# Message products inside the edge batches, node rows fetched per edge type

## The reference

```python
Ks, Qt, Vs = (K[src], Q[tgt], V[src])
for t in range(ET):
    mask = edge_types == t
    Ke = jnp.einsum('ehd,dk->ehk', Ks, Wa[t])
    Ve = jnp.einsum('ehd,dk->ehk', Vs, Wm[t])
    scores = jnp.sum(Ke * Qt, -1) * inv_sqrt_dk * relation_pri[t]
    scores = jnp.where(mask[:, None], scores, -jnp.inf)
    w = jax.nn.softmax(scores, axis=0)
    msgs = msgs + jnp.where(mask[:, None, None], w[..., None] * Ve, 0.0)
agg = jax.ops.segment_sum(msgs.reshape(-1, OUT_DIM), tgt, num_segments=n)
out = agg + node_features      # then a layer norm over the 256 features
```

## Time and profile before

| | us |
|---|---|
| three runs | 1167.97, 1186.32, 1187.55 |
| median | 1186.32 |
| profiled execution, time | 1167.97 |
| its span, first to last instruction | 1167.3 |

### The profile page before, as it was taken

One profiled execution on the slowest core, in us unless ns is written; L12 is line 12 of the kernel. 1 busy time (PEld: TensorE's weight loads), 2 busy tenths in 40 slices (PEclk: granted clock), 3 DMA queues, 4 the chain that ended last, 5 costly groups with the idle time before them and its releaser, 6 DMA issues.

```text
span 1167.3 us, 18084 instructions
## 1 busy us (share of the span) xinstructions
PE 967.1 (83%) x5053; PEld 677.5 (58%) x5053; DVE 803.3 (69%) x1708; ACT 587.4 (50%) x1534; POOL 640.5 (55%) x818
## 2 busy tenths in 40 slices
PE   5989999997157788777877878778778898999998
PEld 4767777775034444444444444444444687888886
DVE  7755888885256777777767677776767677887541
ACT  2657999983234554555545455554555322322220
POOL 4516788886725666666656666565664025664000
PEclk9999999999565766666667666666776799999999
DMA  9722544444736776766767767677674274210020
GB/s 294 220 71 104 159 145 145 146 146 174 234 114 182 208 212 210 205 204 203 214 202 214 210 198 211 201 211 208 201 211 146 69 226 152 79 46 19 1 86 25
DMA packets 112091, 189.89 MB, mean 163 GB/s; under 512 B 18187, under 2 KB 80734, under 8 KB 111990
## 3 DMA queue, kind: packets, MB, share of 16 engines
q0 software_dynamic: 38992, 129.87, 36.1%
q1 hardware_dynamic: 69718, 55.57, 15.7%
q10 hardware_dynamic: 3280, 3.28, 0.8%
HBM read 154.21 MB, written 34.44 MB: 162 GB/s over the span
## 4 chain that ended last, share of the span: by engine, by line
PE 55%; ACT 12%; issue 11%; another core or an unknown queue 10%; DVE 9%; DMA 1%; SPq 1%; POOL 0%; DVEq 0%; ACTq 0%; POOLq 0%
PE ps L2364 7%; PE ps L1621 7%; PE ps L2351 7%; PE ps L1604 6%; PE ps L921 4%; ACT edge L1500 4%; PE ps L2315 3%; PE ps L932 2%; PE ps L909 2%; PE ps L960 2%; ACT edge L1488 2%; PE ps L985 2%; ACT edge L1485 1%; PE ps L1639 1%
## 5 line engine op out<-in xcount | busy, mean ns | idle before, releaser
L1425 POOL DMA_INDIRECT big<-kv_scratch,src_i x336 | 317.8, 946 | 203.0 <-issue 89.8
L1604 PE MATMUL ps<-edge 64*128 64x256 f32 x784 | 177.6, 595 | 39.0 <-issue 38.8
L1750 DVE TENSOR_TENSOR big<-big,ps 128x1024 f32<-128x1024 f32 x84 | 101.6, 1210 | 121.3 <-PE ps L1604 61.9
L1621 PE MATMUL ps<-big,edge 128*64 128x256 f32 x672 | 149.4, 590 | 19.3 <-issue 10.3
L1604 PEld LDWEIGHTS ps<-edge 64*128 64x128 f32 x784 | 104.7, 289 | 89.5 <-issue 75.1
L1522 ACT ACTIVATE edge<-ps 128x256 f32<-128x256 f32 x98 | 37.6, 383 | 213.3 <-remote 146.0
L1621 PEld LDWEIGHTS ps<-big,edge 128*64 128x64 f32 x672 | 63.2, 199 | 78.6 <-issue 70.0
L1500 ACT ACTIVATE edge<-edge 128x64 f32<-128x64 f32 x392 | 102.9, 334 | 0.0
L1757 DVE TENSOR_REDUCE ps<-big 128x32 f32<-128x1024 f32 x84 | 102.3, 1218 | 0.1
L1809 DVE TENSOR_TENSOR big<-big,ps 128x1024 f32<-128x1024 f32 x84 | 98.9, 1209 | 0.0
L2351 PE MATMUL ps<-big 128*128 128x256 f32 (+2 forms) x416 | 88.7, 368 | 2.8 <-ACT big L2264 2.8
(11 more groups left out here) (354 smaller groups left out, 1919.0 us busy)
## 6 DMA issues: line engine op xcount, KB each, us to landing
edge<-q_scratch SPq DMA_DIRECT2D x196, 64.0 KB
...
```

The costliest lines, as they stand in the source:

```text
L1425: pool.indirect_dma_start(kv_slots[s][:, k, :], None, kv_d[0:N, :], bass.IndirectOffsetOnAxis(ap=src_i[:, e:e + 1], axis=0)).then_inc(got[ ...
L1604: ins = pe.matmul(qr_ps[g % 2][:, (2 * hg + k) * D:(2 * hg + k + 1) * D], ohT[64 * hg:64 * hg + 64, g % 2, k * P:(k + 1) * P], qwin[64 * h ...
L1621: ins = pe.matmul(sums_of(g)[64 * hg:64 * hg + 64, :], oneh[:, s, k, hg * 64:hg * 64 + 64], kv_slots[s][:, 2 * hg + k, D:2 * D], start=(k ...
L1750: dve.tensor_tensor(k_rows, k_rows, qr_ps[g % 2].rearrange("p (k d) -> p k d", d=D), ALU.mult).then_inc(pr, 1)
```

## The change

- Ring of 6 slots, all in `big`. `messages` writes to a buffer of its own in `wmix` (two groups) and waits for the sums of g-2; `window_sums` reads it. `rows_of(g)` waits for the messages of g-6 and the sums of g-7.
- Keys lie in HBM by half, and one load serves two batches: 2 DMAs of 64 partitions, 2 KB in one piece each, in place of 2 per batch with pieces of 512 B.
- `ustore` goes. Three groups' turned sums lie in one of two buffers; PE multiplies them with `Wm[t]` in the loop, types 0 and 1 in one step of 4 matmuls and type 2 in another of 2; ACT copies each step and stores 126 rows of 768 (three types, unscaled) to `products_scratch` from its own queue.
- Mixing rows, feed-forward weights and the first `xn` rows are loaded in the loop, one load per batch from batch 8. At batches 43 to 45 the batch of each node is stored, spread to 49 partitions and marked.
- After the last edge PE brings the factors (batch, type, head) to nodes (25 small matmuls). The products stage goes. Heads and tails are loaded as rows of 3 KB, scaled and summed over the types on DVE (`scaled_halves`), then summed on PE, copied and stored as before, to `totals_scratch`.
- In the closing POOL gathers two rows per node, 3 KB of products and 1 KB of totals, and adds the totals to `xn` (`add_totals`); DVE scales the 768 and adds the three types (`scaled_rows`, `two_types`, `three_types`).

```diff
@@ sizes and scratch
-RING = 7
-RING_BIG = RING - 1
+RING = 6
+RING_BIG = RING
+KV_AT = 24696
+MRING = 2
 QRING = 4
-KRING = 2
+KRING, KB = 2, 2
...
-UN, CG = 6, 3
+KEY_PARTS = [(hg, at, min(P, ET // 2 - at)) for hg in range(2) for at in range(0, ET // 2, P)]
+CG = 3
...
+LOADS = 4 + len(MIX_PARTS) + 6
+FIRST = 512 // (ETY * H)
+LOAD_AT, BATCH_AT = 8, 43
...
-    agg_d = scratch("agg_scratch", (AR, D))
+    sum_d = scratch("products_scratch", (PR, PW))
+    tot_d = scratch("totals_scratch", (1 + NHG, D))
+    bat_d = scratch("batch_scratch", (P, NT))
     v_d = scratch("edge_v_scratch", (NB, P, BT * D))
-    key_d = scratch("key_scratch", (ET, P), BF16)
+    key_d = scratch("key_scratch", (2, ET // 2, P), BF16)
@@ buffers
-        ustore = big.take(NG, C, 2 * KW)
...
+        u_buf = big.take(2, C, CG * 2 * KW)
+        p_buf = big.take(2, PW)
...
+        msg = wmix[:, :].rearrange("p (s k d) -> p s k d", s=MRING, k=EG)
@@ where the chunk steps fall
+            def steps_at(g):
+                return [s for s in range(2 * (NCK - 3)) if CG * (s // 2) + 4 + s % 2 == g]
@@ SP in the edge loop
-                def keys(b):
-                    if not in_range(2 * b):
-                        return
-                    s = b % KRING
-                    at_least(sp, ab, 2 * (b - KRING) + 2)
-                    rows_b = key_d[BT * b:BT * (b + 1), :].rearrange("(u h k) c -> h u (k c)", u=2, h=2)
+                def keys(j):
+                    n = min(KB, NB - KB * j)
+                    if n <= 0:
+                        return
+                    s = j % KRING
+                    at_least(sp, ab, 2 * KB * (j - KRING + 1))
                     for hg in range(2):
-                        sp.dma_start(keyr[64 * hg:64 * hg + 64, s, :, :], rows_b[hg:hg + 1, :, :].to_broadcast([64, 2, 2 * P])
-                                     ).then_inc(kin[s], 16)
+                        rows_j = key_d[hg:hg + 1, EG * KB * j:EG * (KB * j + n), :].rearrange("h e c -> h (e c)")
+                        sp.dma_start(keyr[64 * hg:64 * hg + 64, s, 0:2 * n, :].rearrange("p u j -> p (u j)"),
+                                     rows_j.to_broadcast([64, n * EG * P])).then_inc(kin[s], 16)
...
+                    if b % KB == 1:
+                        keys(b // KB + 1)
                     q_window(2 * b)
                     q_window(2 * b + 1)
+                    if b == BATCH_AT:
+                        store_batches(1)
+                    if b == BATCH_AT + 1:
+                        spread_batches(1)
+                    if 0 <= b - LOAD_AT < len(parts):
+                        load_part(b - LOAD_AT)
@@ POOL in the edge loop
                 def rows_of(g):
                     s = g % RING
-                    at_least(pool, yd, g - RING + 1)
+                    at_least(pool, ms, g - RING + 1)
+                    at_least(pool, yd, g - RING)
@@ ACT in the edge loop
                 def keep_sums(g):
                     if not in_range(g):
                         return
+                    ck, at = g // CG, g % CG * 2 * KW
+                    at_least(act, pp, 2 * (ck - 1))
                     act.wait_ge(ud, g + 1)
-                    act.activation(ustore[:, g, :, :].rearrange("p c (g k) -> p c g k", g=2),
+                    act.activation(u_buf[:, ck % 2, :, at:at + 2 * KW].rearrange("p c (g k) -> p c g k", g=2),
                                    sums_of(g).rearrange("p (c g k) -> p c g k", c=C, g=2)[:, :, :, 0:KW], ACT.Copy
                                    ).then_inc(ue, 1)
+
+                def keep_part(n, slot, half):
+                    if half == 0:
+                        return act.activation(p_buf[0:n, slot, 0:2 * D], ps[0][0:n, :], ACT.Copy)
+                    return act.activation(p_buf[0:n, slot, 2 * D:3 * D], ps[0][0:n, 0:D], ACT.Copy)
+
+                def keep_products(step):
+                    ck, half = step // 2, step % 2
+                    act.wait_ge(pp, step + 1)
+                    if half == 0:
+                        at_least(act, p_st[ck % 2], 16 * (ck // 2))
+                    keep_part(columns(ck), ck % 2, half).then_inc(pk, 1)
+                    if half == 1:
+                        store_products(ck)
...
+                def store_products(ck):
+                    n, at = columns(ck), W_AT + ck * CR
+                    act.wait_ge(pk, 2 * ck + 2)
+                    act.dma_start(sum_d[at:at + n, :], p_buf[0:n, ck % 2, :]).then_inc(p_st[ck % 2], 16)
...
                     keep_sums(2 * b - 4)
                     if b >= 0:
                         distances(2 * b + 2)
+                    for step in steps_at(2 * b - 4):
+                        keep_products(step)
                     keep_rows(2 * b - 3)
                     exponentials(b - 1)
                     onehots(2 * b)
                     keep_sums(2 * b - 3)
                     distances(2 * b + 3)
+                    for step in steps_at(2 * b - 3):
+                        keep_products(step)
                     keep_rows(2 * b - 2)
                     onehots(2 * b + 1)
@@ PE in the edge loop
-                                            kv_slots[s][:, 2 * hg + k, D:2 * D], start=(k == 0), stop=(k == 1))
+                                            msg[:, g % MRING, 2 * hg + k, :], start=(k == 0), stop=(k == 1))
...
+                def multiply(to, u, n, types):
+                    for j, t in enumerate(types):
+                        for ch in range(C):
+                            ins = pe.matmul(to[0:n, (j * C + ch) * P:(j * C + ch + 1) * P],
+                                            u[:, ch, 0:n * ETY].rearrange("p (m t) -> p m t", t=ETY)[:, :, t],
+                                            bd_m[:, t, :], start=True, stop=True)
+                    return ins
+
+                def products_by_type(step):
+                    ck = step // 2
+                    pe.wait_ge(ue, CG * ck + chunk_groups(ck))
+                    at_least(pe, pk, step)
+                    multiply(ps[0], u_buf[:, ck % 2, :, :], columns(ck), ((0, 1), (2,))[step % 2]).then_inc(pp, 1)
...
                     target_rows(2 * b + 1)
                     turn_sums(2 * b - 4)
+                    for step in steps_at(2 * b - 4):
+                        products_by_type(step)
                     turn_maxima(b - 1)
                     window_sums(2 * b - 3)
                     spread_maxima(b - 1)
                     turn_sums(2 * b - 3)
+                    for step in steps_at(2 * b - 3):
+                        products_by_type(step)
                     totals(b - 1)
                     target_rows(2 * b + 2)
                     window_sums(2 * b - 2)
...
+                def factors_of_nodes(k):
+                    pe.wait_ge(s_inb, k)
+                    of_tile = in_batch[0:NB, :].rearrange("b (p t) -> b p t", t=NT)
+                    for t in range(NT):
+                        v, j = fac_ps[t // FIRST], t % FIRST
+                        ins = pe.matmul(v[:, j * TH:(j + 1) * TH], of_tile[:, :, t], facT[0:NB, :], start=True, stop=True)
+                        if t in (FIRST - 1, NT - 1):
+                            ins.then_inc(s_fp, 1)
@@ DVE in the edge loop
+                    at_least(dve, yd, g - MRING + 1)
                     v = kv_slots[g % RING][:, :, D:2 * D].rearrange("p k (h d) -> p k h d", d=DK)
-                    dve.tensor_tensor(v, v, wgt[:, g // 2 % 2, (g % 2) * EG * H:(g % 2 + 1) * EG * H]
+                    dve.tensor_tensor(msg[:, g % MRING, :, :].rearrange("p k (h d) -> p k h d", d=DK), v, wgt[:, g // 2 % 2, (g % 2) * EG * H:(g % 2 + 1) * EG * H]
...
+                def mark_batches(k):
+                    dve.wait_ge(s_batin, 16 * k)
+                    dve.tensor_scalar(in_batch[0:NB, :], in_batch[0:NB, :], iota_n[0:NB, :], None, ALU.is_equal).then_inc(s_inb, 1)
@@ closing, SP
+                sp.wait_ge(s_facT, 1)
+                for i in range(2):
+                    sp.wait_ge(p_st[i], 16 * ((NCK + 1 - i) // 2))
+                sp.dma_start(heads[0:HW, :, :], sum_d[W_AT:PR, :].rearrange("(m p s) d -> s p m d", m=2, s=WN)[0]
+                             ).then_inc(s_heads, 16)
...
+                    sp.wait_ge(s_totalk, m + 1)
+                    sp.dma_start(tot_d[1 + m * HW:1 + (m + 1) * HW, :], total[0:HW, m, :]).then_inc(s_totalst, 16)
@@ closing, POOL
+                def add_totals(t):
+                    if t >= NT:
+                        return
+                    k = t % GR
+                    pool.wait_ge(tg_in[k], 16 * (t // GR + 1))
+                    if t < GR:
+                        pool.wait_ge(s_loaded, 16 * LOADS)
+                    else:
+                        pool.wait_ge(xn_in[k], 16 * (t // GR))
+                    pool.tensor_tensor(xn[:, k, :], xn[:, k, :], tg[:, k, :], ALU.add).then_inc(xt, 1)
...
                 load_tails(0)
-                pool.wait_ge(sc_first, EARLY_AT)
```

(87 more changed lines are left out.)

589 lines of the change are left out of this document (316 added, 273 removed).

## The result

| | before | changed |
|---|---|---|
| median | 1178.93 (4 runs, 1167.97 to 1187.55) | 1326.05 (4 runs, 1323.55 to 1331.44) |
| profiled span | 1167.3 | 1324.3 |
| granted clock of TensorE | 0.806 | 0.809 |

The changed kernel is slower: ratio 1.1338, 95% interval 1.1291 to 1.1385. The ratio is taken over fast runs alone, which for the kernel before are 1167.97 and 1171.54. The sign was forecast, the size not: 1326 lies above the range's 1275. What happened is the case that I had given 0.2, and 1326 lies above that case's 1305 too.

What follows compares the result with a forecast made beforehand. It took a cycle of waits as the bound, with PE's news held back during POOL's gather runs. 1167.3 + 34 (loop) - 5 (start) + 7 (closing) = 1203.3, plus 0.7 around the span: 1204 us, range 1115 to 1275.

Steps and rivals of the forecast that it cites:

- the case that I had given 0.2: Edge loop: rival in which every run of gathers holds PE's spread maxima; period 14 to 15, 1260 to 1305 us, chance 0.2.
- The bound: Edge loop: a cycle of waits, PE's news held until about 2 us after a run's last gather; period 12.05 us.
- The run of gathers moves to the end of the first messages: Edge loop: the added message wait shifts POOL's 10 us run from the batch's start to its end.
- between 12.2 and 14.9 I take 12.9, nearer to the lower: Edge loop: period chosen between unheld and held spread maxima, against 12.05 over some 40 batches: +34 us.
- The lower end: Edge loop: the case with spread maxima not held, 12.2 us per batch.
- its sign of being right: Edge loop: among the signs that would confirm the forecast, periods alternating about 12 to 15 us.
- Products in the loop: Edge loop: PE's added matmuls, 1.0 to 2.0 us per batch, have room; their price is inside the period chosen.
- Transfers: Edge loop: 258 KB more per batch, 0.9 us at full engines; counted as nothing, at most 44 us kept for the range.
- Start: Start of the loop: POOL fills the ring with 24 gathers in place of 28, -5 us.
- Closing: Closing stage: 18 us gained before the first turn, +25 us for slower pairs of tiles; net +7, from -8 to +20.
- the 37: Closing: summed way from last products to the first tile's turn, 37 us against some 55 before.
- always holds the spread maxima: Edge loop: rival in which the run always delays PE's spread maxima; +90 to +135, total 1260 to 1305 us, chance 0.2.

Runs made afterwards that it cites:

- h1: Kernel before, with gathers of group g also waiting for the messages of g-6, on a chip where the kernel before takes 1167.6: 1296.1 us.
- r2: Changed kernel, unedited, on a chip where the kernel before takes 1049.1: 1083.2 us.
- c1: Changed kernel without GpSimd's two 128x256 additions of totals per pair of tiles in the closing: 1323.3 us.
- c2: Changed kernel without DVE's second addition over the edge types in the closing: 1327.1 us.
- e4: Changed kernel with gathers waiting for the sums of g-6 and products stored twice: 1142.7 us, where the kernel before takes 1048.0.

## Why the prediction was wrong

- **The bound** was read rightly for chips that hold: h1 follows the argument, 11.8 us to the spread maxima as forecast and 3.4 in place of 3.1 behind them. What the profile of before could not show is that not every chip holds: on others the loop is at GpSimd's 10.0 and the kernel takes 1048.
- **The run of gathers moves to the end of the first messages**: right (668.88, 684.05).
- **The step that failed** is "between 12.2 and 14.9 I take 12.9, nearer to the lower": +34 us forecast, +137.5 measured, 15.3 against 12.15 per batch. The lower end needed the spread maxima to pass, at 5.9 us into the run by my own sum; in the trace even the turned maxima at 4.2 are held for 3.2 us. Nor do periods alternate about 12 and 15, as its sign of being right had it: of the 43, four are 12.8 to 13.9 and the rest 14.2 to 16.7. The 12.9 was a mean over four early batches with the gathers in different places. In the one of 15.0 us they had begun 4.0 us ahead of the products at 352.26 and went on without a long gap, as the new order has them begin ahead; in most of the others they came in fours with gaps of 1.4 us, which the new order doesn't have. The row to price with was the one of 15.0, and it stood in the text as the rival's evidence. With 3 us over 45 batches the sum is 1168+135-5+7 = 1305, above the range's 1275.

```profile
348.25 0.94 POOL L1425 DMA_INDIRECT big<-kv_scratch,src_i  x1 [1.43 <-remote]
```

- **Products in the loop**: hidden, as counted. All that the change puts into the loop is 0.15 us per batch in r2; on the chip of h1, whose loop takes 701.0 us from the second to the last batch, the changed kernel's loop takes 712.4 in c1 and 709.3 in c2. What the products cost by sitting ahead of the maxima no run separates.
- **Transfers**: nothing was counted, up to 44 kept. The same pairs leave 8 to 11 us in the whole loop for transfers and products together. The Trainium skill's rule that DMAs of all issuing engines share the same 16 engines ("DMA: Bandwidth & Descriptors", "Issuing engines are not separate DMA queues") agrees with e4, 0.38 us per batch for more stores from ScalarE's queue beside GpSimd's gathers, though e4 doesn't show that the DMA engines are where they meet.
- **Start**: -5 forecast, -2.8 measured.
- **Closing**: +7 forecast with 20 as the upper end, +22.2 measured. The way to the first turn gained 11.4 (77.0 to 65.6 after the last batch's products) and not 18. Of the terms that made up the 37, the scaling of heads and tails took 6.3 and not 3.1 (the sum had one of the two), their totals on PE another 6.0 and not 3.6, and the first tile's chain to its turn 9.9 (1088.80 to 1098.67) and not 4; others came out shorter, and together they are 43. The 25 matmuls that bring the factors to nodes, 12.07 us, I had left out: they end at 1069.15, and PE's totals start at 1070.19, 2.2 us after the first scaled rows they need. So they cost 2 us at most there. The pair is 12.0 and not 11.0: in the pair shown GpSimd's four gathers take 5.2, as counted, but its four roots 4.5 and not 3.6, and the two additions with their wait 2.1 and not 1.4. First to last turn +33.1 against +25.
- **The rivals**: "always holds the spread maxima", 1260 to 1305 at 0.2, was the case; with the closing at +20 it gives 1318, still 8 short. What is missing is the period (15.29, not 15.0), the start and the closing's last 2 us.
